# A fused decoder layer on one core: the causal mask of the score maxima added in row tiles, small VectorE steps in one-input forms, and the gate's last step on GpSimd

## The chip, the cores and the metric

The kernel runs on one core of one Trainium2 chip. The metric is the device time of one execution in microseconds. TensorE (PE), VectorE (DVE), ScalarE (ACT), GpSimd (POOL) and SyncE (SP, which only starts DMAs here) each run their own list of instructions in order and meet through semaphores.

## What is computed

64 sequences of 256 tokens with 256 features go through three attention layers and a gated feed-forward layer. All arithmetic is float32.

```
x = x + local_attention(layernorm(x))            # 16 heads of 16; a token sees its 7 neighbours
x = x + cross_attention(layernorm(x), ctx)       # keys and values: 120 rows of ctx
x = layernorm(x)
# decoder block:
a = einsum('bhqd,bhkd->bhqk', q, k) * hd ** -0.5         # q, k, v from rmsnorm(x, n1)
a = softmax(where(triu(ones, 1), -1e9, a))               # causal: no key later than the query
x = x + (a @ v) @ o_w.T
gp = softmax(xf @ gate_w.T); ew = top_k(gp, 2)           # xf = rmsnorm(x, n2)
ew = ew / (sum(ew) + 1e-9)
x = x + silu(xf @ up_w.T) @ down_w.T * sum(ew)
```

## The kernel before

One sequence at a time would leave the engines waiting for each other, so five sequences (LANES) are in work together. `sequence_parts` lists the parts of one sequence with an engine, an assumed duration and predecessors. `Plan` runs through all 64 sequences on a clock of its own with these durations and fixes three things before the program is built: the order of parts on each engine, which of four single PSUM banks (SINGLES) or of the one group of four banks (QUADS) each part fills, and the count that each wait needs. On the chip only the order and the waits remain. A changed duration, or a part on another engine, can therefore move parts that the edit does not name. In the steady state the order repeats once per sequence.

Parts that the text needs, with their lines:

- **Local layer, window path.** PE projects rows k, v, q (`project_rows`, L635), DVE adds biases (L1044), SP sends the rows to DRAM and fetches them back in windows of shifted tokens (`k_windows`, `v_windows`). POOL multiplies queries with windows in six k-chunks (L987), DVE reduces each (L1057), `window_max` (L1065 to L1069) centres them, ACT takes the exponent, `window_sum` (L1074 to L1077) normalises; then six v-chunks on POOL (L992).
- **Maxima.** The softmax needs each query's largest score. `max` fills the group of four banks with scores, one bank for each of the four row tiles of 32 contraction rows (L670; each matmul has a 32-row tile of TensorE to itself, so four run side by side), and DVE reduces them (L1100). For the causal layer (L677) a bfloat16 matmul of the identity with `causal_mask` adds -1e30 to later keys of the diagonal 128x128 block before the reduction. There are three fills per sequence: one of 128 queries with all 16 heads (512 columns of mask per bank), two of the other 128 queries with 8 heads each (256 columns).
- **`round_max`** (L1107 to L1109) splits the maxima into two bfloat16 parts, PE turns them (`shift`, L687), and `scores` (L700, L708) computes the scores again, keys by queries, with the maxima subtracted. ACT takes the exponent (L873), POOL zeroes later keys (`scores` on POOL, L1003), PE multiplies with the values (L731), `untangle` (L742, DVE L1117 and L1118) divides by the sums.
- **`turn_out`** (L756) transposes the attention result, ACT copies it (L898), `project_out` (L765) multiplies by the output weights, DVE adds it to x (L1129).
- **Feed-forward.** `gate` (PE L774, DVE L1133 to L1139, ACT L904, L906), `up` in four pieces (PE L784, ACT L917, DVE L1145), `weigh` (L1152 to L1156: sum of the two top weights over their sum plus 1e-9), `down` (PE L793, DVE L1161). `turn` (L617, ACT L834) transposes a normed input.

Every part that fills a bank waits until the engine that drains the bank's previous content is through. `settle` makes DVE or POOL wait for its own previous result.

## Time and profile before

| | before |
|---|---|
| median of 3 runs | 4210.85 us (4209.32 to 4218.56) |
| the profiled execution's own time | 4207.72 us |
| its span in the trace | 4206.0 us |
| busy share PE, DVE, ACT, POOL | 94%, 65%, 44%, 57% |
| TensorE's granted clock | 0.987 of full speed |

The span is the time from the first to the last traced instruction, 1.7 us less than that execution's own time, which in turn lies 3.1 us below the median. Busy shares are means over the whole span; with five sequences in flight an engine can be busy nearly all the time while what sets the pace runs through other engines.

### The profile page before, as it was taken

The page shows a single profiled execution, that of the slowest core. Times are in us where ns is not written, and L with a number is a line of the kernel's source. Part 1 is how long each engine was busy: PE and PEld are TensorE (multiplying, and loading weights), DVE is VectorE, ACT ScalarE, POOL GpSimd, SP SyncE. Part 2 cuts the span into 40 slices and gives each one's busy share as a digit, 9 for nine tenths or more (in the row PEclk, how much of TensorE's full clock was granted, in tenths as well). Part 3 has the DMA queues.
Part 4 walks back from the last instruction along what each step waited for, and adds up shares of the span by engine and source line. Part 5 has one row for each costly group of instructions (what it writes and reads, how often), then busy time and mean ns, then how long its engine had stood idle before and what let it go on. Part 6 is the DMA issues. An engine that isn't in the chain of part 4 may idle for free.

```text
span 4206.0 us, 92442 instructions
## 1 busy us (share of the span) xinstructions
PE 3943.8 (94%) x38016; PEld 3128.5 (74%) x38016; DVE 2745.3 (65%) x5137; ACT 1849.0 (44%) x3393; POOL 2402.4 (57%) x2898
## 2 busy tenths in 40 slices
PE   4699999999999999999999999999999999999997
PEld 4477777777777777777777777777777777777776
DVE  4666666666666766766766766766766766766742
ACT  1344444444444444444444444444444444444442
POOL 4655655655655655655655655655655556556521
PEclk9799999999999999999999999999999999999999
DMA  4111111111111111111111111111111111111100
GB/s 146 47 42 64 39 57 64 39 57 62 36 61 53 43 64 45 51 64 43 53 64 41 55 64 41 56 64 39 58 64 39 58 64 39 57 64 39 57 7 8
DMA packets 87125, 221.25 MB, mean 53 GB/s; under 512 B 8316, under 2 KB 53688, under 8 KB 70328
## 3 DMA queue, kind: packets, MB, share of 16 engines
q1 hardware_dynamic: 86712, 215.34, 14.3%
q8 instruction: 309, 5.06, 0.5%
q14 instruction: 104, 0.85, 0.1%
HBM read 164.92 MB, written 50.39 MB: 51 GB/s over the span
## 4 chain that ended last, share of the span: by engine, by line
PE 54%; POOL 18%; DVE 14%; DMA 7%; issue 3%; ACT 2%; SPq 0%; POOLq 0%; DVEq 0%
POOL chunks L987 11%; PE ps L793 11%; PE ps L651 9%; DMA k_windows<-passed_k 7%; PE ps L700 6%; PE ps L635 5%; PE ps L731 5%; PE ps L784 5%; PE ps L670 4%; DVE nmax L1100 3%; PE ps L617 3%; POOL x L960 2%; PE ps L657 2%; DVE nmax_parts L1107 2%; POOL x L965 2%
## 5 line engine op out<-in xcount | busy, mean ns | idle before, releaser
L992 POOL TENSOR_TENSOR chunks<-v_windows,xT 128x560 f32<-128x560 f32 (+1 forms) x384 | 868.0, 2277 | 386.5 <-DVE xT L1077 264.8
L1100 DVE TENSOR_REDUCE nmax<-ps 128x16 f32<-128x1920 f32 (+2 forms) x320 | 714.7, 2234 | 419.7 <-PE ps L670 283.2
L987 POOL TENSOR_TENSOR chunks<-rest,k_windows 128x512 f32<-128x512 f32 (+1 forms) x384 | 554.8, 1453 | 691.9 <-DMA k_windows<-passed_k 684.6
L873 ACT ACTIVATE prob<-ps 120x1024 f32<-120x1024 f32 (+1 forms) x512 | 619.7, 1236 | 739.2 <-PE ps L708 738.6
L784 PE MATMUL ps<-xT,w_up 128*128 128x256 f32 x2048 | 505.7, 391 | 58.7 <-ACT xT L834 44.0
L1003 POOL TENSOR_SCALAR_AFFINE_SELECT prob<-prob 128x512 f32<-128x512 f32 x512 | 314.0, 639 | 386.1 <-ACT prob L873 386.1
L784 PEld LDWEIGHTS ps<-xT,w_up 128*128 128x128 f32 x2048 | 377.8, 192 | 145.2 <-ACT xT L834 57.0
L793 PE MATMUL ps<-w_down,held 128*128 128x256 f32 x2048 | 459.1, 382 | 2.2 <-DVE held L1145 2.2
L1057 DVE TENSOR_REDUCE xT<-chunks 128x32 f32<-128x512 f32 (+1 forms) x384 | 293.4, 764 | 253.9 <-POOL chunks L987 248.7
L1057 DVE TENSOR_REDUCE held<-chunks 128x80 f32<-128x560 f32 (+1 forms) x384 | 296.2, 771 | 242.7 <-POOL chunks L992 237.7
L793 PEld LDWEIGHTS ps<-w_down,held 128*128 128x128 f32 x2048 | 383.8, 190 | 62.2 <-issue 9.4
L917 ACT ACTIVATE rest<-ps 128x512 f32<-128x512 f32 x256 | 152.7, 597 | 604.1 <-PE ps L784 604.1
L700 PE MATMUL ps<-held 32*120 32x256 f32 (+2 forms) x6144 | 391.1, 368 | 18.3 <-ACT prob L873 12.9
L670 PE MATMUL ps<-held 32*128 32x256 f32 (+2 forms) x8192 | 374.1, 313 | 20.8 <-DVE nmax L1100 8.3
L700 PEld LDWEIGHTS ps<-held 32*120 32x120 f32 (+1 forms) x6144 | 284.9, 184 | 137.8 <-issue 128.6
L670 PEld LDWEIGHTS ps<-held 32*128 32x128 f32 x8192 | 285.5, 187 | 83.4 <-issue 62.3
L731 PE MATMUL ps<-prob,va 120*32 120x256 f32 (+2 forms) x6144 | 332.1, 348 | 12.0 <-POOL prob L1003 3.3
L1035 DVE BATCH_NORM_STATS2 stats<-x 128x6 f32<-128x256 f32 x384 | 143.9, 417 | 231.9 <-DMA x<-in_x 229.8
L898 ACT COPY xT<-ps 128x512 f32<-128x512 f32 x128 | 74.9, 585 | 446.1 <-PE ps L756 446.1
L731 PEld LDWEIGHTS ps<-prob,va 120*32 120x32 f32 (+1 forms) x6144 | 185.0, 109 | 114.4 <-issue 61.2
L617 PE MATMUL ps<-ident,held 128*128 128x128 f32 x1024 | 165.1, 285 | 30.0 <-ACT held L829 15.7
L617 PEld LDWEIGHTS ps<-ident,held 128*128 128x128 f32 x1024 | 114.5, 142 | 96.4 <-issue 60.3
(139 smaller groups left out, 6889.6 us busy)
## 6 DMA issues: line engine op xcount, KB each, us to landing
k_windows<-passed_k SPq DMA_DIRECT2D x64, 1024.0 KB, 4.8
v_windows<-passed_v SPq DMA_DIRECT2D x64, 1024.0 KB, 6.9
...
```

The lines of the kernel that those rows point to most:

```text
L617: last = nc.tensor.transpose(ps[:, b, col:col + P], xn[s][:, tb, k * P:(k + 1) * P], ident[:])
L651: last = nc.tensor.matmul(ps[:, b, m * n:(m + 1) * n], wt[:, k, m * P:(m + 1) * P], src[:, k, 0:n], start=(k == 0), stop=(k == 1))
L670: last = nc.tensor.matmul(ps[:, first + r, place * keys:(place + 1) * keys], qT[s][e][rows, m, tb * P:(tb + 1) * P], kT[s][rows, m, 0:keys ...
L700: nc.tensor.matmul(ps[0:keys, first + r, n * T + col:n * T + col + qs], kT[s][rows, m, key0:key0 + keys], qT[s][e][rows, m, q0:q0 + qs], s ...
L731: last = nc.tensor.matmul(ps[SLOT * j:SLOT * (j + 1), b, e * T + q0:e * T + q0 + qs], va[s][0:keys, kb, head:head + SLOT], pr[0:keys, j, c ...
L784: last = nc.tensor.matmul(ps[:, b, m * T:(m + 1) * T], w_up[:, k, (2 * m2 + m) * P:(2 * m2 + m + 1) * P], xT[s][:, k, :], start=(k == 0), ...
L793: last = nc.tensor.matmul(ps[:, b, tb * D:(tb + 1) * D], hid[s][:, m, tb * P:(tb + 1) * P], w_down[:, m, :], start=(m == 0), stop=(m == F ...
L873: last = nc.scalar.activation(dst[0:keys], ps[0:keys, first:first + 4, n * T:n * T + dst.shape[2]], ACT.Exp, scale=SCALE)
L987: last = nc.gpsimd.tensor_tensor(chunk_of(c).rearrange("p (j d) -> p j d", d=D), q_row, window("k", (b + first) * D, (D, n), (1, D)), ALU. ...
L992: last = nc.gpsimd.tensor_tensor(chunk_of(c).rearrange("p (h i j) -> p h i j", i=HD, j=WINDOW), window("v", b * D + first * HD, (HD, n), ( ...
L1057: nc.vector.tensor_reduce(to, chunk_of(c).rearrange("p (x i) -> p x i", i=width), AX_X, ALU.add).then_inc(reduced[s], 1)
L1100: nc.vector.tensor_reduce(dst, src, AX_X, ALU.max, negate=True).then_inc(emptied[b], 1)
```

## The change

Five edits:

1. The mask of the maxima is added in row tiles. In setup PE builds two tables, `pick_rows` and `mask_rows`, which hold for each slab of 32 queries the selecting matrix and the mask's rows, repeated in each of the four row groups; DVE copies them out of PSUM as bfloat16. In a causal fill, each slab (0 to 3) and each row tile issue one matmul with 32 contraction rows, over the keys from 32 x slab on: 128, 96, 64 and 32 keys per head in place of 128 for every query.
2. `round_max` uses three reductions over an axis of length one (or two) in place of a cast, a subtraction and a cast. The gate's negation becomes such a reduction too.
3. `weigh` moves from DVE to POOL, with four instructions in place of five: fac = t * (t + 1e-9 z) ** -1. `down` on DVE waits for it through a new semaphore.
4. The durations that `Plan` assumes: 1.38 and 1.12 for PE in a causal fill (before 1.72 and 1.29), and `weigh` as 1.2 on POOL (before 0.9 on DVE).
5. Setup work: POOL makes one more 512-column pattern, PE eight matmuls, DVE two copies of 512 columns.

```diff
-                pe = 0.85 if layer == CROSS else 1.72 if tb == 0 else 1.29
+                pe = 0.85 if layer == CROSS else 1.38 if tb == 0 else 1.12
...
-    weighed = part("weigh", (), "DVE", 0.9, [a])
+    weighed = part("weigh", (), "POOL", 1.2, [a])
...
+            @block.tensor
+            def _(pe):
+                pe.wait_ge(setup_pool, 16)
+                for b, src in ((0, ident_b), (1, causal_mask)):
+                    for slab in range(4):
+                        last = nc.tensor.matmul(ps[:, b, slab * P:(slab + 1) * P], like_rows[:, slab, :], src[:],
+                                                start=(slab == 0), stop=(slab == 3), skip_group_check=True)
+                last.then_inc(setup_pe, 1)
...
-                dve.wait_ge(setup_dve, 24)
+                dve.wait_ge(setup_pe, 1)
+                for b, dst in ((0, pick_rows), (1, mask_rows)):
+                    nc.vector.tensor_copy(dst[:].rearrange("p s q -> p (s q)"), ps[:, b, :]).then_inc(setup_dve, 1)
+                dve.wait_ge(setup_dve, 26)
...
                         if L == CAUSAL:
-                            for r in range(4):
-                                to = ps[:, first + r, 0:2 * len(ms) * keys].rearrange("p (g k) -> p g k", k=keys)
-                                last = nc.tensor.matmul(to[:, :, tb * P:(tb + 1) * P], ident_b[:],
-                                                        causal_mask[:, 0:2 * len(ms), :], start=False, stop=True,
-                                                        skip_group_check=True)
+                            for slab in range(4):
+                                for r in range(4):
+                                    rows = slice(32 * r, 32 * r + 32)
+                                    to = ps[:, first + r, 0:2 * len(ms) * keys].rearrange("p (g k) -> p g k", k=keys)
+                                    later = mask_rows[rows, slab, 32 * slab:P].unsqueeze(1)
+                                    last = nc.tensor.matmul(to[:, :, tb * P + 32 * slab:(tb + 1) * P],
+                                                            pick_rows[rows, slab, :],
+                                                            later.to_broadcast([32, 2 * len(ms), P - 32 * slab]),
+                                                            start=False, stop=True, tile_position=(32 * r, 0),
+                                                            skip_group_check=True)
                         last.then_inc(filled[b], 1)
...
+                    elif name == "weigh":
+
+                        pool.wait_ge(exps_ready[s], reached["exps_ready", "gate", seq, ()])
+                        settle(nc.gpsimd.tensor_scalar(fac_r[s][:], zsum[s][:], 1e-9, None, ALU.mult))
+                        settle(nc.gpsimd.tensor_tensor(fac_r[s][:], tsum[s][:], fac_r[s][:], ALU.add))
+                        settle(nc.gpsimd.tensor_tensor(fac_r[s][:], fac_r[s][:], neg_one[:], ALU.pow))
+                        nc.gpsimd.tensor_tensor(fac[s][:], tsum[s][:], fac_r[s][:], ALU.mult).then_inc(weighed[s], 1)
                 for s in range(LANES):
+                    pool.wait_ge(weighed[s], plan.total["weighed", s])
...
                         hi, lo = half_max(s)[:, :, 0:4], half_max(s)[:, :, 4:8]
-                        whole = nmax[s][:].rearrange("p b (r g) -> p (b r) g", g=4)
-                        left = nmax_rest[s][:].rearrange("p b (r g) -> p (b r) g", g=4)
-                        settle(nc.vector.tensor_copy(hi, whole))
-                        settle(nc.vector.tensor_tensor(left, whole, hi, ALU.subtract))
-                        nc.vector.tensor_copy(lo, left).then_inc(nmax_ready[s], 1)
+                        whole, less = (nmax_pair[s][:, n].rearrange("p b (r g) -> p (b r) g", g=4) for n in range(2))
+                        both = nmax_pair[s][:].rearrange("p n b (r g) -> p (b r) g n", g=4)
+                        with nc.allow_low_precision(reason="the second part holds what the first one rounds off"):
+                            settle(nc.vector.tensor_reduce(hi, whole.unsqueeze(3), AX_X, ALU.max))
+                            settle(nc.vector.tensor_reduce(less, hi.unsqueeze(3), AX_X, ALU.max, negate=True))
+                            nc.vector.tensor_reduce(lo, both, AX_X, ALU.add).then_inc(nmax_ready[s], 1)
                     elif name == "shift":
...
-                        nc.vector.tensor_scalar(ntop[s][:], top[s][:, :, 0], -1.0, None,
-                                                ALU.mult).then_inc(tops_ready[s], 1)
+                        nc.vector.tensor_reduce(ntop[s][:], top[s][:, :, 0:1], AX_X, ALU.max,
+                                                negate=True).then_inc(tops_ready[s], 1)
...
-                    elif name == "weigh":
-
-                        dve.wait_ge(exps_ready[s], reached["exps_ready", "gate", seq, ()])
-                        settle(nc.vector.reciprocal(fac_r[s][:], zsum[s][:]))
-                        settle(nc.vector.tensor_tensor(fac[s][:], tsum[s][:], fac_r[s][:], ALU.mult))
-                        settle(nc.vector.tensor_scalar(zsum[s][:], fac[s][:], 1e-9, None, ALU.add))
-                        settle(nc.vector.reciprocal(fac_r[s][:], zsum[s][:]))
-                        settle(nc.vector.tensor_tensor(fac[s][:], fac[s][:], fac_r[s][:], ALU.mult))
                     elif name == "down":
                         b = bank(name, seq, args)
                         dve.wait_ge(biased[s], reached["biased", "norm", seq, (3,)])
+                        dve.wait_ge(weighed[s], reached["weighed", "weigh", seq, ()])
```

The planner's numbers move parts. Three places show it, with one turn of the repeating order picked out (a number behind a name is the lane's or buffer's, as in xT2); the line numbers of the change are higher by 26 to 40 (PE: L696 is the former L670, L706 L677, L773 L742, L805 L774, L815 L784, L787 L756, L796 L765, L643 L617, L683 L657, L677 L651, L731 L700, L739 L708, L762 L731).

First TensorE, at the last causal fill of a sequence and the feed-forward of the one ahead of it. Before:

```order
L670 MATMUL ps<-held1 128x256 x8
L677 MATMUL ps<-causal_mask,ident_b 128x2x128 x4
L742 MATMUL ps<-ident,rest2 128x128 x4
L774 MATMUL ps<-w_gate,xT0 128x8 x4
L784 MATMUL ps<-xT0,w_up 128x256 x4
L756 MATMUL ps<-ident,held2 128x128 x4
L765 MATMUL ps<-w_cross_o,xT2 128x256 x4
L784 MATMUL ps<-xT0,w_up 128x256 x4
L617 MATMUL ps<-ident,held3 128x128 x4
L784 MATMUL ps<-xT0,w_up 128x256 x4
L687 MATMUL ps<-ident_b,nmax_parts1 128x128 x2
```

and with the change:

```order
L696 MATMUL ps<-held1 128x256 x8
L706 MATMUL ps<-mask_rows,pick_rows 128x2x128 x4
L706 MATMUL ps<-mask_rows,pick_rows 128x2x96 x4
L706 MATMUL ps<-mask_rows,pick_rows 128x2x64 x4
L706 MATMUL ps<-mask_rows,pick_rows 128x2x32 x4
L773 MATMUL ps<-ident,rest2 128x128 x4
L805 MATMUL ps<-w_gate,xT0 128x8 x4
L815 MATMUL ps<-xT0,w_up 128x256 x4
L787 MATMUL ps<-ident,held2 128x128 x4
L815 MATMUL ps<-xT0,w_up 128x256 x4
L796 MATMUL ps<-w_cross_o,xT2 128x256 x4
L643 MATMUL ps<-ident,held3 128x128 x4
```

The mask is sixteen small matmuls; the third piece of `up` now stands ahead of `project_out` (w_cross_o), directly behind `turn_out`.

Second VectorE, from the end of `window_max` to `round_max`. Before:

```order
L1069 TENSOR_TENSOR xT2<-xT2,nmax2 128x224
L1117 RECIPROCAL rsum0<-ps 128x16
L1118 TENSOR_TENSOR held0<-ps,rsum0 128x256
L1074 TENSOR_REDUCE rsum2<-xT2 128x32
L1076 RECIPROCAL rsum2<-rsum2 128x32
L1077 TENSOR_TENSOR xT2<-xT2,rsum2 128x224
L1117 RECIPROCAL rsum0<-ps 128x16
L1118 TENSOR_TENSOR held0<-ps,rsum0 128x256
L1100 TENSOR_REDUCE nmax4<-ps 128x4x2
L1145 SCALAR_TENSOR_TENSOR held3<-rest3,ps 128x512
L1107 CAST nmax_parts4<-nmax4 128x8x4
L1108 TENSOR_TENSOR nmax_rest4<-nmax4,nmax_parts4 128x32
```

and with the change:

```order
L1108 TENSOR_TENSOR xT2<-xT2,nmax_pair2 128x224
L1157 RECIPROCAL rsum0<-ps 128x16
L1158 TENSOR_TENSOR held0<-ps,rsum0 128x256
L1139 TENSOR_REDUCE nmax_pair4<-ps 128x4x2
L1157 RECIPROCAL rsum0<-ps 128x16
L1158 TENSOR_TENSOR held0<-ps,rsum0 128x256
L1113 TENSOR_REDUCE rsum2<-xT2 128x32
L1115 RECIPROCAL rsum2<-rsum2 128x32
L1116 TENSOR_TENSOR xT2<-xT2,rsum2 128x224
L1147 TENSOR_REDUCE nmax_parts4<-nmax_pair4 128x8x4
L1148 TENSOR_REDUCE nmax_pair4<-nmax_parts4 128x32
L1149 TENSOR_REDUCE nmax_parts4<-nmax_pair4 128x8x4
```

The reduction of the last causal fill (nmax_pair4<-ps 128x4x2) now runs ahead of the second `untangle` and ahead of `window_sum`; `up` (held<-rest,ps) has gone behind `round_max`.

Third TensorE, behind `down`, from the turn of the next causal layer on. Before:

```order
L617 MATMUL ps<-ident,held2 128x128 x4
L756 MATMUL ps<-ident,held4 128x128 x4
L657 MATMUL ps<-w_cross_v,y4 120x256 x2
L700 MATMUL ps<-held1 128x256 x4
L700 MATMUL ps<-held1 128x128 x4
L708 MATMUL ps<-nmaxT1,pick 128x256 x4
L708 MATMUL ps<-nmaxT1,pick 128x128 x4
L731 MATMUL ps<-prob0,va1 32x256 x4
L731 MATMUL ps<-prob0,va1 32x128 x4
L731 MATMUL ps<-prob1,va1 32x256 x4
L731 MATMUL ps<-prob1,va1 32x128 x4
L700 MATMUL ps<-held1 128x256 x4
```

and with the change:

```order
L643 MATMUL ps<-ident,held2 128x128 x4
L683 MATMUL ps<-w_cross_v,y4 120x256 x2
L731 MATMUL ps<-held1 128x256 x4
L731 MATMUL ps<-held1 128x128 x4
L739 MATMUL ps<-nmaxT1,pick 128x256 x4
L739 MATMUL ps<-nmaxT1,pick 128x128 x4
L677 MATMUL ps<-xT2,w_causal_q 128x256 x4
L731 MATMUL ps<-held1 128x256 x4
L731 MATMUL ps<-held1 128x128 x4
L739 MATMUL ps<-nmaxT1,pick 128x256 x4
L739 MATMUL ps<-nmaxT1,pick 128x128 x4
L762 MATMUL ps<-prob0,va1 32x256 x4
```

`turn_out` of the local layer (L756) has left this place (it now stands behind the first causal fill and its `project_out`), and the projection w_causal_q, which stood behind the last scores, stands ahead of them; the `values` (prob,va) come after all four scores.

## Rows read from the trace of the kernel before

**Rows 1.** The page: busy time by engine; chain that ended last by line.

```profile
PE 3943.8 (94%) x38016; PEld 3128.5 (74%) x38016; DVE 2745.3 (65%) x5137; ACT 1849.0 (44%) x3393; POOL 2402.4 (57%) x2898
...
POOL chunks L987 11%; PE ps L793 11%; PE ps L651 9%; DMA k_windows<-passed_k 7%; PE ps L700 6%; PE ps L635 5%; PE ps L731 5%; PE ps L784 5%; PE ps L670 4%; DVE nmax L1100 3%; PE ps L617 3%; POOL x L960 2%; PE ps L657 2%; DVE nmax_parts L1107 2%; POOL x L965 2%
```

**Rows 2.** Chain of waits, one turn around 2000 us: start, duration (us), what.

```profile
1991.56 1.93 PE ps L635 x8
...
1996.86 4.73 DMA k_windows<-passed_k
...
2016.83 0.40 DVE xT L1065
...
2020.65 2.28 DVE nmax L1100
...
2023.53 1.42 DVE nmax_parts L1107
...
2026.12 0.64 PE ps L617 x4
...
2027.48 1.97 PE ps L784 x8
...
2054.42 1.93 PE ps L635 x8
```

**Rows 3.** Timeline of all engines, 2013 to 2034 us: start, duration, instruction, idle before.

```profile
2018.76 0.53 DVE L1074 TENSOR_REDUCE rsum<-xT 128x32 f32<-128x224 f32 x1
...
2020.02 0.25 DVE L1117 RECIPROCAL rsum<-ps 128x16 f32<-128x16 f32 x1
...
2020.88 0.63 PE L756 MATMUL ps<-ident,held 128*128 128x128 f32 x4
...
2022.28 1.97 PE L765 MATMUL ps<-w_cross_o,xT 128*128 128x256 f32 x8 [0.77 <-ACT xT L898]
...
2026.65 0.68 DVE L1129 TENSOR_TENSOR x<-x,ps 128x512 f32<-128x512 f32 x1
...
2029.28 0.28 PE L687 MATMUL ps<-ident_b,nmax_parts 128*128 128x128 bf16 x2
2029.36 0.73 POOL L939 TENSOR_TENSOR rstd<-ms,neg_half 128x2 f32<-128x2 f32 x1
...
2029.64 1.97 PE L651 MATMUL ps<-xT,w_cross_q 128*128 128x256 f32 x8
...
2032.19 2.53 DVE L1156 TENSOR_TENSOR fac<-fac,fac_r 128x2 f32<-128x2 f32 x1
```

**Rows 4.** Timeline of TensorE, 2059 to 2072 us.

```profile
2062.28 1.04 PE L677 MATMUL ps<-causal_mask,ident_b 128*128 128x512 bf16 x4
2063.15 1.89 PE L765 MATMUL ps<-w_causal_o,xT 128*128 128x256 f32 x8
...
2067.66 0.40 PE L708 MATMUL ps<-nmaxT,pick 32*120 32x256 bf16 x8
2067.99 1.99 PE L657 MATMUL ps<-w_causal_v,xT 128*128 128x256 f32 x8
```

**Rows 5.** Timeline of all engines, 2034 to 2057 us.

```profile
2041.19 0.60 PE L756 MATMUL ps<-ident,held 128*128 128x128 f32 x4
...
2041.63 1.03 PE L657 MATMUL ps<-w_cross_v,y 128*120 128x256 f32 x4
...
2043.81 1.51 PE L731 MATMUL ps<-prob,va 128*32 128x256 f32 x32
...
2046.46 1.45 ACT L873 ACTIVATE prob<-ps 128x1536 f32<-128x1536 f32 x1 [0.50 <-PE ps L708]
...
2047.98 1.22 POOL L1003 TENSOR_SCALAR_AFFINE_SELECT prob<-prob 128x512 f32<-128x512 f32 x2 [1.51 <-ACT prob L873]
...
2048.38 1.26 ACT L846 ACTIVATE held<-ps,half 128x512 f32<-128x512 f32 x2 [0.47 <-PE ps L651]
```

**Rows 6.** The first cast of `round_max`, line L1107: duration min/median/max (ns).

```profile
L1107 DVE CAST nmax_parts<-nmax x128: 168/173/1791, 116.4 to 4137.0; 128x32 bf16<-128x32 f32 x128
```

41 lines of the change are left out of this document (27 added, 14 removed).

## The prediction

> **What bounds the kernel now.** I start on the page. TensorE is busy 94% of the span, VectorE 65%, GpSimd 57% [rows 1]. That invites the reading that every nanosecond taken from TensorE shortens the run. The page's chain contradicts it: its largest entry is GpSimd's window chunks (L987, 11%), and the fetch of k_windows has another 7% [rows 1]. So I follow the chain of waits over one turn of the repeating order. From one start of project_rows for k (L635, 1991.56) to the next (2054.42) are 62.86 us [rows 2]. I cut the turn into three stretches:
>
> - **Stretch 1**, 1991.56 to 2016.83, 25.27 us: project k, DMA out, the fetch (4.73 us), six k-chunks on GpSimd with other GpSimd work between them, up to window_max (L1065) [rows 2]. All but the first two microseconds is not TensorE.
> - **Stretch 2**, 2016.83 to 2027.48, 10.65 us: VectorE through window_max, untangle, window_sum, untangle, the reduction of 2.28 us, the stalled cast (1.42 us), then turn (L617), a copy, and the last `up` (L784) [rows 2].
> - **Stretch 3**, 2027.48 to 2054.42, 26.94 us: TensorE without interruption, from `up` over `down` to the next project_rows [rows 2].
>
> Two of the three causal fills lie in stretch 1 by time, the third at the seam to stretch 2. In all of them TensorE runs beside the chain. That places the change: the mask is cheaper where TensorE is not on the path, and only what moves in stretches 2 and 3 counts. The order printed for both kernels repeats in 58 of 64 turns, so I multiply by 58.
>
> **The mask itself.** Before, four matmuls of 512 columns take 2063.15 - 2062.28 = 0.87 us, 0.22 each [rows 4]: 0.42 ns per column. In row tiles four matmuls run side by side: eight of 256 columns (L708), two rounds, take 2067.99 - 2067.66 = 0.33 us including the switch back to the undivided array [rows 4]. Two rounds of 256 at 0.42 ns are 0.22, so the switch costs 0.11. New 16-head fill: (512+384+256+128) columns x 0.42 = 0.54 us, plus the switch, now behind the mask and not ahead of it. Saved: 0.33. New 8-head fill: 640 columns, 0.27, against 0.43: saved 0.16, twice. Unknown is whether rounds of 128 and 64 columns keep that rate. Bounds: if each short round costs a full 256-column round (0.11 us), the 8-head fill takes 0.44 and saves nothing, and the 16-head fill still saves 0.28. I take 0.03 us per fill off for the shortest round, about 0.55 us per sequence in all. On the chain it is worth zero in my main case; its cover is TensorE's slack ahead of turn_out, worked out below as about 0.9 us. Without the cover it would be 0.55 x 64 = 35 us.
>
> The Trainium skill (TensorEngine Tiling (Array Packing), Performance Considerations) says a matmul has about 60 cycles of overhead, so very short ones gain nothing. By it the 64-column round is at its floor, and my 0.03 would be nearly nothing; no sum here changes.
>
> **round_max and the gate.** The cast takes 0.17 us at the median and up to 1.79 [rows 6], 1.42 in this turn [rows 2]; GpSimd's v-chunks run at that time. The three reductions are near the uncontended 0.2 us, 0.65 with their waits: 1.2 us less on VectorE in stretch 2. If reductions stalled too, round_max would stay at 1.85 us. The Trainium skill (SBUF — State Buffer, Who interferes with whom) says that a cast can take the port pair shared with GpSimd and then blocks, while `tensor_reduce` never contends. By that rule the stall is gone, by the other bound it stays; which of the two hardly moves the end, as the next part shows.
>
> **Stretch 2 with the new order.** Let W be window_max's start. VectorE before: window_max and the first untangle to W + 1.93 (window_sum starts 2018.76), window_sum 1.26 (to 2020.02), second untangle, and TensorE's turn_out at 2020.88, W + 4.05 [rows 3]. After: the reduction, about 2.20 from start to start (2.28 busy [rows 2]), stands there and window_sum behind. turn_out comes 2.20 - 1.26 = 0.94 later, W + 4.99. This is the late step of the new order. From turn_out on: copy on ScalarE until 2022.28, 1.40 [rows 3]; then the third `up`, 1.80, project_out, 1.73 (estimates, from the 1.93 of project k's eight matmuls [rows 2] less 0.1 to 0.2 for the switch there), and turn, 0.44 like its twin turn_out [rows 5]. So the last `up` starts at W + 10.36, with no wait: its bank was drained by the second `up`, no longer by project_out's addition, which ran at 2026.65 to 2027.33 [rows 3] and was what it waited for before, along with the 1.4 us copy. Before: W + 10.65. Gain 0.29 us. project_out's own bank needs the first `up` on VectorE, now behind round_max: ready at W + 7.4, needed at W + 8.2. With stalled reductions W + 8.6, and 0.4 of the gain is lost.
>
> **Stretch 3.** turn_out of the local layer leaves it: 2041.63 - 2041.19 = 0.44 [rows 5]. It goes to stretch 1, where TensorE has slack. The shift-to-projection seam (2029.28 to 2029.64, 0.36 for two short transposes [rows 3]) waited for the third `up` on VectorE; its bank now comes from `turn`: 0.25 less. Two restarts behind waits are gone with it, an estimate of 0.15 from the same 0.1 to 0.2. Against this: w_causal_q used to run between the last scores and the next fill of the four banks and hid the exponent (1.45 us [rows 5]). Now `values` does (1.51 [rows 5]), but ScalarE first evicts q (1.26 [rows 5]), so the banks come free about 0.4 us later than TensorE wants them; then `values` waits some 0.15 for GpSimd's masking (1.22 [rows 5]) of the last scores. Net 0.84 - 0.55 = 0.29 less.
>
> **Stretch 1.** GpSimd has the same parts in slightly different order: nothing. ScalarE's norm there is 0 to 0.3 us tighter; I take 0.
>
> **weigh.** VectorE loses five small instructions, the last of which stalled 2.53 us [rows 3], behind the last `up`, ahead of nothing on the chain. On GpSimd four take at most 0.73 each (the power, L939 [rows 3]), about 1.5 us, between v-chunks, which also start 2.8 us later (behind window_sum). GpSimd's wait for the k_windows fetch absorbs it; queued behind it are the maskings of the scores, and these have about 1.9 us of room before `values`.
>
> **Sum.** (0.29 + 0.29) x 58 = 34 us less. Setup adds two copies of 512 columns on VectorE at its end, 0.68 each like L1129 [rows 3]: 1.4 more. The tail, where one sequence runs alone, gains about 2. Together 34: own time 4207.7 - 34 = 4173.7, and with the median 3 above it about 4177.
>
> **Rivals.**
> - *TensorE is the bound after all* (20%). For it: 94% busy. Against: the chain leaves it for 36 of 63 us. Then mask and stretch gains add: (0.55 + 0.58) x 60 = 68 us, 4143. The Trainium skill (Perfetto Trace Analysis, Identifying the Most-Contended Engine) has this rule: the engine with the highest occupancy is the one to optimise first.
> - *More than that* (5%): fewer stalls let stretch 1 shrink; 4110.
> - *Nothing is left* (15%): ScalarE's norm in stretch 1 (0.3) and the exponent behind the q eviction (0.3 more than I count) eat both gains: 4203 to 4219.
> - *Slower* (18%): turn_out is 0.94 later, and the rest of stretch 2 does not give it back, because the last `up` still waits for a drain on VectorE. Then 0.94 - 0.29 = 0.65 x 58 = 38 us more, 4249. It decides once the wait there keeps more than 0.65 of its former 0.9.
> - *My case* (42%): 4177, own range 4150 to 4200.
>
> The range reaches from 4120 to 4240 and leaves out under 2 in 10. A measurement of this kernel tells about 0.2%, 8.4 us, from no change. Faster by more: 42 + 20 + 5, less a few at the edge, 65%; within: 16%; slower: 19%.
>
> **What would show it.** In the trace after: turns of 62.3 us; turn_out at W + 5.0; the third `up` after a wait of 0.77 for turn_out's copy; no wait of the last `up` behind L643; first reduction of round_max near 0.2 us; 16-head masks of 0.54 to 0.65 us; stretch 1 unchanged at 25.3. I am wrong if stretch 1 changes, if GpSimd's maskings arrive late at `values`, or if the last `up` waits at W + 11.

## The result and the profile after

The changed kernel takes 4175.45 us at the median of 4 runs (4169.04 to 4178.95), beside 4211.02 us of the kernel before on the same chip (4 runs, 4209.32 to 4218.56): ratio 0.991, 95% interval 0.9893 to 0.9928. The forecast was 4177 us. The profiled execution took 4175.73 us with a span of 4174.0. The total was met, in part by luck: the turns gained less than forecast, and the first sequences gained what no term had. The runs below also show that two of the prediction's readings were not right.

The page of the kernel after (busy time by engine; the chain that ended last by line), beside [rows 1]:

```profile
PE 3876.1 (93%) x40328; PEld 3131.7 (75%) x40328; DVE 2518.5 (60%) x4820; ACT 1848.0 (44%) x3393; POOL 2488.5 (60%) x3156
...
POOL chunks L1018 12%; PE ps L824 11%; PE ps L677 9%; DMA k_windows<-passed_k 7%; PE ps L815 6%; PE ps L661 5%; ACT prob L904 5%; PE ps L731 4%; DVE nmax_pair L1139 4%; PE ps L696 4%; PE ps L796 3%; PE ps L762 3%; POOL x L991 2%; POOL x L99
```

TensorE is busy 68 us less in all (the mask alone takes 38 of that, see mask only) and still 93% of a shorter span. The chain still has the window chunks first. New on it is ScalarE's exponent (L904) with 5%.

The chain of waits over one turn after, with the events of [rows 2]:

```profile
1971.02 1.93 PE ps L661 x8
...
1976.32 4.79 DMA k_windows<-passed_k
...
1996.37 0.40 DVE xT L1104
...
2033.49 0.64 PE ps L661 x2
```

A turn is 62.47 us here, 62.86 before. The fetch and the six k-chunks that make up stretch 1 are as they were.

TensorE's timeline after (start, duration, instruction) with the masks, beside [rows 4]:

```profile
1978.77 0.72 PE L706 MATMUL ps<-mask_rows,pick_rows 32*128 32x512 bf16 x16
1979.42 1.99 PE L796 MATMUL ps<-w_causal_o,xT 128*128 128x256 f32 x8
...
1996.44 0.46 PE L706 MATMUL ps<-mask_rows,pick_rows 32*128 32x256 bf16 x16
1996.82 0.66 PE L773 MATMUL ps<-ident,rest 128*128 128x128 f32 x4
```

The 16-head mask takes 1979.42 - 1978.77 = 0.65 us, the 8-head mask 0.38. In the prediction's terms 0.54 + 0.11 and 0.27 + 0.11: the short rounds keep the rate of the long ones.

The timeline of all engines in stretch 2 after, beside [rows 3]. window_max starts at W = 1996.37:

```profile
2001.36 0.63 PE L787 MATMUL ps<-ident,held 128*128 128x128 f32 x4 [0.86 <-DVE held L1158]
...
2002.39 0.18 DVE L1147 TENSOR_REDUCE nmax_parts<-nmax_pair 128x32 bf16<-128x32 f32 x1
2002.60 0.19 DVE L1148 TENSOR_REDUCE nmax_pair<-nmax_parts 128x32 f32<-128x32 bf16 x1
2002.64 4.72 POOL L1023 TENSOR_TENSOR chunks<-v_windows,xT 128x672 f32<-128x672 f32 x2 [7.02 <-DVE xT L1116]
...
2002.76 1.97 PE L815 MATMUL ps<-xT,w_up 128*128 128x256 f32 x8 [0.77 <-ACT xT L929]
...
2002.96 0.68 DVE L1185 SCALAR_TENSOR_TENSOR held<-rest,ps 128x512 f32<-128x512 f32 x1
...
2004.56 1.89 PE L796 MATMUL ps<-w_cross_o,xT 128*128 128x256 f32 x8
...
2006.29 0.60 PE L643 MATMUL ps<-ident,held 128*128 128x128 f32 x4
...
2006.72 1.89 PE L815 MATMUL ps<-xT,w_up 128*128 128x256 f32 x8
```

turn_out stands at W + 4.99, the third `up` at W + 6.39 after a wait of 0.77, project_out at W + 8.19, turn at W + 9.92, the last `up` at W + 10.35 without a wait. The first cast's successor (L1147) takes 0.18 us and ends 0.07 ahead of GpSimd's first v-chunk (2002.64); the second reduction (L1148) runs into that chunk and takes 0.19. Over the whole trace:

```profile
L1147 DVE TENSOR_REDUCE nmax_parts<-nmax_pair x128: 174/177/186, 118.8 to 4103.8; 128x32 bf16<-128x32 f32 x128
L1148 DVE TENSOR_REDUCE nmax_pair<-nmax_parts x128: 185/186/188, 119.0 to 4104.1; 128x32 f32<-128x32 bf16 x128
```

L1147 stands in the place of the line in [rows 6], whose longest was 1791 ns. By itself it doesn't show that a reduction escapes the stall, since by start times and durations only 4 of the 128 overlap with a GpSimd instruction. Of L1148 64 do, with the same 188 ns at most, and of the first reduction in forms only (below) 63 do, with 181 ns at most.

Stretch 3 after, beside [rows 5]:

```profile
2024.37 1.26 ACT L877 ACTIVATE held<-ps,half 128x512 f32<-128x512 f32 x2 [0.47 <-PE ps L677]
...
2025.53 1.45 ACT L904 ACTIVATE prob<-ps 128x1536 f32<-128x1536 f32 x1
...
2027.12 1.17 PE L696 MATMUL ps<-held 32*128 32x120 f32 x32 [0.32 <-ACT prob L904]
...
2028.52 1.51 PE L762 MATMUL ps<-prob,va 128*32 128x256 f32 x32 [0.23 <-POOL prob L1034]
```

TensorE waits 0.32 us for the four banks behind the last exponent and 0.23 for GpSimd's masking: the two waits that the prediction had put at 0.4 and 0.15. The exponent (to 2026.98) had to wait for q's eviction, as the prediction said.

Over many turns the same cuts give the following table. It is worked out from start times in each trace, as means over turns 8 to 57 of the repeating order: "to chunk" is from project_rows k to the first k-chunk, "chunks" from there to W. Means are longer than the typical turn, since the fetch of k_windows takes up to 3 us more in some.

| kernel | median us, ratio to before (95%) | turn | to chunk | chunks | W to last `up` | last `up` to rows |
|---|---|---|---|---|---|---|
| before | | 63.39 | 10.77 | 15.08 | 10.64 | 26.87 |
| after | 4175.45, 0.991 (0.9893 to 0.9928) | 62.93 | 10.74 | 15.10 | 10.38 | 26.70 |
| mask only | 4207.37, 0.9995 (0.9986 to 1.0003) | 63.40 | 10.77 | 15.09 | 10.64 | 26.88 |
| old mask | 4166.70, 0.9902 (0.9888 to 0.9915) | 62.73 | 10.50 | 15.19 | 10.34 | 26.70 |
| mask twice | 4188.05, 0.9934 (0.9919 to 0.995) | 63.11 | 10.66 | 15.40 | 10.34 | 26.70 |
| forms only | 4132.76, 0.9822 (0.9809 to 0.9835) | 62.12 | 10.77 | 15.09 | 9.41 | 26.84 |
| old forms | 4255.44, 1.0104 (1.009 to 1.0118) | 64.28 | 10.65 | 15.12 | 11.80 | 26.70 |
| untangle first | 4135.96, 0.9803 (0.9784 to 0.9823) | 62.21 | 10.66 | 15.10 | 9.73 | 26.70 |
| order only | 4466.98, 1.06 (1.0584 to 1.0615) | 67.79 | 10.62 | 15.17 | 11.76 | 30.22 |
| weigh planned | 4318.63, 1.0266 (1.0249 to 1.0283) | 65.31 | 10.71 | 15.11 | 10.42 | 29.07 |
| weigh back | 4173.99, 0.9903 (0.9889 to 0.9917) | 62.86 | 10.67 | 15.11 | 10.37 | 26.70 |
| numbers back | 4157.78, 0.9878 (0.9862 to 0.9893) | 62.50 | 10.51 | 15.10 | 9.40 | 27.49 |
| tight | 4230.11, 1.0053 (1.0039 to 1.0066) | 63.77 | 10.67 | 15.08 | 9.19 | 28.83 |
| mask and forms | 4125.21, 0.9797 (0.9784 to 0.9811) | 62.10 | 10.77 | 15.08 | 9.41 | 26.83 |

By phases the changed kernel gains 8.1 us ahead of the sixth project_rows k (280.0 to 271.9), 25.4 in the turns up to the 64th (3673.7 to 3648.3), and loses 1.6 behind it (252.3 to 253.9).

### The profile page after: what moved, and what is told of

Its sections match the earlier page's. It is cut to its first block, busy times and chain, and to the rows that moved or that the text cites. A ratio compares the mean times of both kernels' runs of the same rounds, so it can differ in the third digit from the quotient of the medians.

```text
span 4174.0 us, 96951 instructions
## 1 busy us (share of the span) xinstructions
PE 3876.1 (93%) x40328; PEld 3131.7 (75%) x40328; DVE 2518.5 (60%) x4820; ACT 1848.0 (44%) x3393; POOL 2488.5 (60%) x3156
## 4 chain that ended last, share of the span: by engine, by line
PE 49%; POOL 20%; DVE 10%; DMA 8%; ACT 7%; issue 4%; SPq 0%; POOLq 0%; DVEq 0%
POOL chunks L1018 12%; PE ps L824 11%; PE ps L677 9%; DMA k_windows<-passed_k 7%; PE ps L815 6%; PE ps L661 5%; ACT prob L904 5%; PE ps L731 4%; DVE nmax_pair L1139 4%; PE ps L696 4%; PE ps L796 3%; PE ps L762 3%; POOL x L991 2%; POOL x L996 2%; PE ps L643 1%
## 5 line engine op out<-in xcount | busy, mean ns | idle before, releaser
L1139 DVE TENSOR_REDUCE nmax_pair<-ps 128x16 f32<-128x1920 f32 (+2 forms) x320 | 715.2, 2235 | 514.8 <-PE ps L696 353.0
L904 ACT ACTIVATE prob<-ps 120x1024 f32<-120x1024 f32 (+1 forms) x512 | 619.6, 1236 | 464.8 <-PE ps L739 464.4
L815 PE MATMUL ps<-xT,w_up 128*128 128x256 f32 x2048 | 509.4, 393 | 74.8 <-ACT xT L929 45.2
L815 PEld LDWEIGHTS ps<-xT,w_up 128*128 128x128 f32 x2048 | 375.5, 193 | 159.5 <-issue 83.3
L731 PE MATMUL ps<-held 32*120 32x256 f32 (+2 forms) x6144 | 391.3, 368 | 29.7 <-ACT prob L904 24.4
L696 PE MATMUL ps<-held 32*128 32x256 f32 (+2 forms) x8192 | 373.8, 313 | 38.8 <-ACT prob L904 24.0
L731 PEld LDWEIGHTS ps<-held 32*120 32x120 f32 (+1 forms) x6144 | 285.1, 184 | 157.3 <-issue 148.0
L696 PEld LDWEIGHTS ps<-held 32*128 32x128 f32 x8192 | 286.1, 187 | 95.7 <-issue 74.4
L762 PE MATMUL ps<-prob,va 120*32 120x256 f32 (+2 forms) x6144 | 332.4, 349 | 17.7 <-POOL prob L1034 17.7
L762 PEld LDWEIGHTS ps<-prob,va 120*32 120x32 f32 (+1 forms) x6144 | 177.0, 110 | 115.7 <-issue 52.3
L853 ACT ACTIVATE held<-x,nmean,rstd 128x256 f32<-128x256 f32 x256 | 140.0, 595 | 181.6 <-POOL nmean L972 180.4
L1185 DVE SCALAR_TENSOR_TENSOR held<-rest,ps 128x512 f32<-128x512 f32 x256 | 175.2, 685 | 37.0 <-ACT rest L948 31.0
```

What stands on the lines that cost most here:

```text
L696: last = nc.tensor.matmul(ps[:, first + r, place * keys:(place + 1) * keys], qT[s][e][rows, m, tb * P:(tb + 1) * P], kT[s][rows, m, 0:keys ...
L731: nc.tensor.matmul(ps[0:keys, first + r, n * T + col:n * T + col + qs], kT[s][rows, m, key0:key0 + keys], qT[s][e][rows, m, q0:q0 + qs], s ...
L762: last = nc.tensor.matmul(ps[SLOT * j:SLOT * (j + 1), b, e * T + q0:e * T + q0 + qs], va[s][0:keys, kb, head:head + SLOT], pr[0:keys, j, c ...
L815: last = nc.tensor.matmul(ps[:, b, m * T:(m + 1) * T], w_up[:, k, (2 * m2 + m) * P:(2 * m2 + m + 1) * P], xT[s][:, k, :], start=(k == 0), ...
L904: last = nc.scalar.activation(dst[0:keys], ps[0:keys, first:first + 4, n * T:n * T + dst.shape[2]], ACT.Exp, scale=SCALE)
L1139: nc.vector.tensor_reduce(dst, src, AX_X, ALU.max, negate=True).then_inc(emptied[b], 1)
```

## The experiments

The diffs are cut to their core. They stand against the changed kernel, that of forms only against the one before. Where a kernel has the old mask (old mask, forms only, order only), GpSimd's pattern and TensorE's eight matmuls of the new setup stay in it, and one copy in place of two makes the wide mask table.

### What the mask is worth

**Mask only.** The planner's numbers, `weigh`, round_max and the gate as before; only the mask and its setup are new. The order of parts is that of before.

```diff
-                pe = 0.85 if layer == CROSS else 1.38 if tb == 0 else 1.12
+                pe = 0.85 if layer == CROSS else 1.72 if tb == 0 else 1.29
...
+                        settle(nc.vector.tensor_copy(hi, whole))
+                        settle(nc.vector.tensor_tensor(less, whole, hi, ALU.subtract))
+                        nc.vector.tensor_copy(lo, less).then_inc(nmax_ready[s], 1)
```

Expected: 

> The row-tile mask alone (with its setup); planner's numbers, weigh and round_max as before, so every engine has the order of before. Chain theory (the mask lies beside the chain in all three fills): the steady turn stays at 62.9 to 63.4 us, setup costs 1.4 to 2.4, start and tail give back 2 to 10; 4209 us, 4200 to 4213. Rival, TensorE is the bound: about 0.55 us per sequence, 4178.

Measured: 4207.37 us, ratio 0.9995. The turn has not moved by 0.02 us in any stretch. TensorE's busy time on the page is 3905.5 us for 3943.8, 0.60 less per sequence, and the kernel takes as long. So the saving is covered in this order, and the rival "TensorE is the bound" falls. The Trainium skill (Perfetto Trace Analysis, Identifying the Most-Contended Engine) says to optimise first the engine with the highest occupancy, and to judge TensorE by the busy share of its weight loads. That is 74% here [rows 1], still the highest, but this edit takes nothing out of it (3140.5 us for 3128.5), so the ratio speaks against the reading by matmul time and leaves the page's own measure untested.

**Old mask.** The changed kernel with the four 128-row matmuls per fill of before; their wide table is copied on VectorE in setup.

```diff
+                            for r in range(4):
+                                to = ps[:, first + r, 0:2 * len(ms) * keys].rearrange("p (g k) -> p g k", k=keys)
+                                last = nc.tensor.matmul(to[:, :, tb * P:(tb + 1) * P], ident_b[:],
+                                                        causal_wide[:, 0:2 * len(ms), :], start=False, stop=True,
+                                                        skip_group_check=True)
```

Expected: 

> The changed kernel in its own order, with the mask added as before (four matmuls of 128 contraction rows). Chain theory: the cover in front of turn_out hides the third fill, but in the new order ScalarE's norm for the GpSimd work of stretch 1 is tight, and the 16-head fill comes 0.33 us later in front of it: up to 0.3 us per turn, 4175 + 10 to 19 = 4185 to 4194. If the mask is wholly hidden: 4175. Rival, TensorE is the bound: 4175 + 35 = 4210.

Measured: 4166.70 us, ratio 0.9902, which overlaps with that of the change. The stretch of chunks is 0.09 us longer; the one ahead of it, with the fetch, varies between any two kernels by as much as here (0.24 shorter). Nothing of the mask's saving can be seen to reach the end in the new order either, where TensorE waits 0.86 us ahead of turn_out (2001.36 above).

**Mask twice.** Every causal fill adds its mask two times, which changes the added value to -2e30.

```diff
-                            for slab in range(4):
+                            for slab in (0, 1, 2, 3, 0, 1, 2, 3):
```

Expected: 

> The changed kernel with the row-tile mask issued twice (adds -2e30 and not -1e30 to later keys): 1.1 us more TensorE work per sequence. Chain theory: the 16-head fill's second half (0.54) delays ScalarE's norm in stretch 1, the 8-head ones (0.27 each) meet the wait of turn_out: 0.5 x 58 = 30 us, 4205, 4195 to 4212. If the mask is wholly hidden: 4175. Rival, TensorE is the bound: 1.1 x 60 = 66, 4241.

Measured: 4188.05 us, 12.6 above the changed kernel; by the ratios it is 10, and the two intervals overlap a little. Of the 1.1 us more per sequence (0.54 + 2 x 0.27, since a second switch isn't needed) the stretch of chunks shows 0.30, more than its spread between the other kernels (15.08 to 15.19). The cover is wider than I expected (4205 us), but it ends.

### What the forms are worth

**Forms only.** Only round_max and the gate's negation have the new forms; mask, planner's numbers and `weigh` are those of before, and so is the order.

```diff
-                            settle(nc.vector.tensor_copy(hi, whole))
-                            settle(nc.vector.tensor_tensor(left, whole, hi, ALU.subtract))
-                            nc.vector.tensor_copy(lo, left).then_inc(nmax_ready[s], 1)
+                            settle(nc.vector.tensor_reduce(hi, whole.unsqueeze(3), AX_X, ALU.max))
+                            settle(nc.vector.tensor_reduce(less, hi.unsqueeze(3), AX_X, ALU.max, negate=True))
+                            nc.vector.tensor_reduce(lo, both, AX_X, ALU.add).then_inc(nmax_ready[s], 1)
```

Expected: 

> Only the one-input forms of round_max and of the gate's negation; mask, weigh, planner's numbers and order of before. Chain theory: the 1.2 us of stall in round_max stand on the chain of before through the second `up` and the bank of `turn`; without them `turn` starts 0.31 us earlier, where TensorE gets there by itself, so 0.31 x 58 = 18 us: 4193, 4188 to 4200. Rival, TensorE is the bound (VectorE is 65% busy): 4211.

Measured: 4132.76 us, 60 below what I expected. The forms alone gain 77 us, more than twice what the whole change does. The timeline of this kernel, W = 1977.88:

```profile
1984.49 0.18 DVE L1132 TENSOR_REDUCE nmax_parts<-nmax_pair 128x32 bf16<-128x32 f32 x1
...
1986.42 0.68 DVE L1154 TENSOR_TENSOR x<-x,ps 128x512 f32<-128x512 f32 x1
...
1986.85 0.60 PE L641 MATMUL ps<-ident,held 128*128 128x128 f32 x4
...
1987.29 1.92 PE L808 MATMUL ps<-xT,w_up 128*128 128x256 f32 x8
1987.55 0.58 ACT L858 COPY xT<-ps 128x512 f32<-128x512 f32 x1
```

The last `up` stands at W + 9.41, 1.24 ahead of before. In [rows 3] project_out's addition ran from W + 9.82, here from W + 8.54: 1.28 earlier, the stall that is gone. So before, the whole stall of the cast stood on the chain: cast, addition, bank, last `up`. The prediction had named the copy of turn's result, 1.4 us with its gaps, as a second thing that the last `up` waited for, and the 0.31 us of my expectation is turn's own gain (W + 8.97 here, W + 9.29 before) passed on through that copy. Here the last `up` starts 0.44 after turn and ahead of that copy (1987.55): it doesn't depend on it.

**Old forms.** The changed kernel with round_max's cast, subtraction and cast.

```diff
-                            settle(nc.vector.tensor_reduce(hi, whole.unsqueeze(3), AX_X, ALU.max))
-                            settle(nc.vector.tensor_reduce(less, hi.unsqueeze(3), AX_X, ALU.max, negate=True))
-                            nc.vector.tensor_reduce(lo, both, AX_X, ALU.add).then_inc(nmax_ready[s], 1)
+                        settle(nc.vector.tensor_copy(hi, whole))
+                        settle(nc.vector.tensor_tensor(less, whole, hi, ALU.subtract))
+                        nc.vector.tensor_copy(lo, less).then_inc(nmax_ready[s], 1)
```

Expected: 

> The changed kernel with round_max as cast, subtraction and cast. As the prediction has it (same stall as before, project_out 0.4 late): 4175 + 23 = 4198. Closer look: round_max now runs just behind window_sum, at the moment GpSimd starts its 2.5 us v-chunk, so the subtraction stalls for the whole chunk, the first `up` leaves its bank 2.3 us later and project_out waits 1.7 us: 4175 + 1.7 x 58 = 4273. Rival, TensorE is the bound: 4175.

Measured: 4255.44 us. Its timeline, W = 1975.90:

```profile
1982.17 4.62 POOL L1023 TENSOR_TENSOR chunks<-v_windows,xT 128x672 f32<-128x672 f32 x2 [7.03 <-DVE xT L1116]
...
1982.35 2.39 DVE L1147 CAST nmax_parts<-nmax_pair 128x32 bf16<-128x32 f32 x1
1984.66 0.68 DVE L1183 SCALAR_TENSOR_TENSOR held<-rest,ps 128x512 f32<-128x512 f32 x1
...
1985.48 1.97 PE L796 MATMUL ps<-w_cross_o,xT 128*128 128x256 f32 x8 [1.22 <-DVE held L1183]
...
1987.72 1.89 PE L815 MATMUL ps<-xT,w_up 128*128 128x256 f32 x8
```

The second cast begins 0.18 us after GpSimd's first v-chunk and ends when that chunk is through, 2.39 us for 0.18 of work. The first `up` on VectorE stands behind it, project_out waits for its bank (1.22), and the last `up` comes at W + 11.8 in place of W + 10.35. The new order has put round_max directly behind window_sum, which releases the v-chunks: without the new forms it is 1% slower than before. The expectation's closer look (4273) had this mechanism, on the subtraction in place of the second cast; its 4198 by the prediction's terms was too low.

### What the new order is worth

**Untangle first.** One swap on VectorE: the cross layer's second `untangle` goes ahead of the last causal reduction.

```diff
+            if dve[i][0] == "max" and dve[i][2] == (CAUSAL, 2) and dve[i + 1][0] == "untangle" and dve[i + 1][2] == (CROSS, 1):
+                dve[i], dve[i + 1] = dve[i + 1], dve[i]
```

Expected: 

> The changed kernel with two neighbouring parts swapped in VectorE's order: the second untangle of the cross layer ahead of the reduction of the third causal fill; all other orders and banks as they are. Chain theory: turn_out no longer waits until W + 5.0 but follows the second `up` at about W + 4.0; project_out is then held by the first `up`'s bank until W + 7.5, so the last `up` starts at W + 9.7 and not W + 10.35: 0.68 us per turn, 4175 - 39 = 4136, 4125 to 4150. Rival, TensorE is the bound: its work is the same, only its waits (0.9) could go: 4175 to 4120 without the stop at 0.68. Rival, the delay of turn_out costs nothing: 4175.

Measured: 4135.96 us. TensorE's timeline, W = 1913.71:

```profile
1919.09 1.97 PE L819 MATMUL ps<-xT,w_up 128*128 128x256 f32 x8 [0.82 <-ACT xT L933]
...
1921.11 1.96 PE L800 MATMUL ps<-w_cross_o,xT 128*128 128x256 f32 x8
...
1923.35 1.89 PE L819 MATMUL ps<-xT,w_up 128*128 128x256 f32 x8
```

The third `up` moves from W + 6.39 to W + 5.38, and the last to W + 9.64. project_out is held until W + 7.40 by the bank of the first `up`. The late turn_out of the new order is thus worth 0.65 us a turn by the means of that stretch and 0.71 in this turn, as expected.

**Order only.** The planner's two numbers are new; mask, forms and `weigh` (VectorE) are those of before.

```diff
-    weighed = part("weigh", (), "POOL", 1.2, [a])
+    weighed = part("weigh", (), "DVE", 0.9, [a])
```

Expected: 

> Only the planner's two numbers for a causal fill are changed: mask, round_max, gate and weigh are those of before, weigh on VectorE. TensorE's and ScalarE's order come out exactly as in the change. Chain theory: the new order has round_max behind window_sum, where the old forms stall behind GpSimd's chunk (2.3 us), weigh stalls ahead of project_out's addition, and the mask is late in front of the norm: 4175 + 98 + 17, more with weigh: 4280 to 4340, so slower than before. Rival, the order is what makes the change fast: about 4185. Rival, TensorE is the bound: 4211.

Measured: 4466.98 us, 6% slower than before; the direction was as expected, the size beyond it. Behind the last `up` are 3.35 us more than before. The timeline there:

```profile
2008.06 2.12 POOL L1016 TENSOR_TENSOR chunks<-v_windows,xT 128x560 f32<-128x560 f32 x1 [1.46 <-DVE held L1081]
2008.13 2.07 DVE L1176 TENSOR_TENSOR fac<-tsum,fac_r 128x2 f32<-128x2 f32 x1
...
2010.83 0.69 DVE L1152 TENSOR_TENSOR x<-x,ps 128x512 f32<-128x512 f32 x1
...
2011.66 2.60 PE L675 MATMUL ps<-xT,w_cross_q 128*128 128x256 f32 x8 [2.13 <-DVE x L1152]
...
2014.19 1.67 PE L724 MATMUL ps<-held 32*128 32x256 f32 x16
...
2023.27 0.94 PE L724 MATMUL ps<-held 32*128 32x256 f32 x16
```

The planner has put `weigh` ahead of project_out's addition. Its first product waits for a v-chunk, and the cross query projection waits 2.13 us behind it. That is the larger part of the 3.35. The rest is TensorE's granted clock. It is 1.00 from 2008.0 to 2011.6, where TensorE is busy 1.53 of 3.6 us, then 0.73 until 2014.3 and 0.83 until 2020.0, a mixture of its two levels, and 1.00 again. At the lower level the same sixteen matmuls (L724) take 1.67 us in place of 0.94, and the projection 2.60 where weigh planned has 1.97. Over the whole run the granted clock is 0.973 here and 0.987 before: 0.027 x 4464 less 0.013 x 4206 is 66 us, an estimate of 1.1 us a turn.

**Weigh planned.** The changed kernel, forms included, with `weigh` in its old instructions on VectorE and the planner told so (the diff above and the five instructions).

Expected: 

> The changed kernel with weigh back on VectorE in its five instructions and the planner told so (0.9 on VectorE). The planner then puts it between the gate and project_out's addition, as in the kernel with the new order alone, where its product stalled 2.07 us behind a v-chunk and the cross query projection on TensorE waited 2.13 us for project_out's addition. The forms of round_max and the gate are the new ones. My theory: the stall of weigh stands on the chain there; the turn is 1.5 to 2.5 us longer than in the changed kernel, 4260 to 4320. Rival, weigh costs nothing wherever it stands, as it did behind the last up: 4175.

Measured: 4318.63 us. Timeline, at the same place:

```profile
2005.52 1.14 DVE L1184 TENSOR_TENSOR fac<-tsum,fac_r 128x2 f32<-128x2 f32 x1
...
2006.69 2.06 DVE L1185 TENSOR_SCALAR zsum<-fac 128x2 f32<-128x2 f32 x1
...
2010.01 1.97 PE L676 MATMUL ps<-xT,w_cross_q 128*128 128x256 f32 x8 [1.95 <-DVE x L1160]
```

Two stalls now, 1.14 and 2.06 us, and TensorE waits 1.95, of 2.37 more than in the changed kernel behind the last `up`; the granted clock, 0.981, is lower here too. With the new numbers the forms alone don't save the kernel; `weigh` has to leave VectorE, or to stand elsewhere:

**Weigh back.** The changed kernel with `weigh`'s five instructions on VectorE, placed by hand directly behind the last `up` and not by the planner.

```diff
+            self.order["DVE"].insert(self.order["DVE"].index(("up", p[1], (3,))) + 1, p)
```

Expected: 

> The changed kernel with weigh back on VectorE in its old five instructions, placed directly behind the last `up`; all other orders as they are. Chain theory: its 3.3 us with the stall have cover on VectorE, and GpSimd's 1.5 us less had cover too: 4175, 4171 to 4180. Rival (VectorE's load sets the pace): up to 3.3 us per sequence, 4175 + 50 or more.

Measured: 4173.99 us, no difference. In this order it is the place of `weigh` that decides, not the engine.

### Put together again

**Numbers back.** The changed kernel with 1.72 and 1.29 again in the planner, and nothing else.

Expected: 

> The changed kernel with the planner's two numbers for a causal fill as before (1.72 and 1.29), all else changed: row-tile mask, one-input forms, weigh on GpSimd. The order of parts is then that of before but for weigh. My theory (the forms gain all of it, the new order gives half back, mask and weigh are worth nothing): as fast as the kernel in which only the forms are changed, about 4131 us (4125 to 4137). Rival, the mask's saving comes out once the stall is gone, because TensorE is then nearer to being the bound: 0.55 x 58 = 32 us less, about 4100. Rival, weigh on GpSimd delays the v-chunks or the maskings in this order: 4140 to 4160.

Measured: 4157.78 us: faster than the changed kernel by 18, not by the 44 expected. The third case held. Timeline at the end of the v-chunks, W = 1984.63:

```profile
2001.92 0.71 POOL L1042 TENSOR_TENSOR fac_r<-fac_r,neg_one 128x2 f32<-128x2 f32 x1
...
2004.05 4.26 POOL L1023 TENSOR_TENSOR chunks<-v_windows,xT 128x560 f32<-128x560 f32 x2
...
2008.35 0.74 DVE L1096 TENSOR_REDUCE held<-chunks 128x80 f32<-128x560 f32 x1 [0.61 <-POOL chunks L1023]
...
2009.14 0.66 PE L787 MATMUL ps<-ident,held 128*128 128x128 f32 x4 [0.43 <-DVE held L1096]
```

Here `weigh` on GpSimd stands ahead of the last two v-chunks. The last ends at W + 23.7 (forms only: W + 22.0), and the local layer's turn_out waits 0.43 for it and has moved behind another projection: last `up` to project_rows is 27.49 us, 0.65 more.

**Mask and forms.** The same with `weigh` on VectorE in its five instructions, so that the order is that of before.

Expected: 

> Row-tile mask, its setup, and the one-input forms; the planner's numbers and weigh (five instructions on VectorE) as before, so that the order of parts is that of before. It differs from the kernel of the forms alone (4132.8 us) by the mask only, and from the kernel with the numbers back (4157.8 us) by weigh only. My theory: the 25 us between those two are weigh's, whose four instructions on GpSimd (1.9 us with their gaps) make the last v-chunk end 23.7 us after window_max in place of 22.0, so that turn_out of the local layer waits on TensorE; the mask is worth nothing in this order too. So 4131 us (4125 to 4138). Rival, the row-tile mask costs something where TensorE waits less: 4150 to 4160. Rival, the mask's 0.55 us a sequence come out now: about 4100.

Measured: 4125.21 us, ratio 0.9797: the lowest of all, though untangle first (0.9803) can't be told from it. So `weigh` on GpSimd costs the kernel above some 33 us by the medians. In the traces, whose spans are 27 apart, it is 23 in the turns and 6.7 behind the 64th project_rows (253.0 to 246.3), with the start 2.8 shorter. Against forms only (0.9822) the median is 7 us lower, with intervals that just touch, and the turns are alike: 62.10 us against 62.12. The start is 3.6 longer, 2.2 of it setup; the end behind the 64th project_rows is 8.9 shorter. That goes with the granted clock. The windows of forms only, near the end (length, busy time of PE, PEld, DVE, ACT, POOL, then PEclk, the granted clock):

```profile
4080.00:4086.00 6.00, 3.46 (x80) 2.47 (x80) 0.81 (x2) 3.49 (x3) 2.00 (x4) 0.97 0.14 45
4086.00:4092.00 6.00, 4.60 (x40) 3.12 (x40) 0.63 (x2) 0.59 (x1) 0.44 (x1) 0.50 0.00 0
4092.00:4100.00 8.00, 5.05 (x13) 3.24 (x12) 2.13 (x6) 0.59 (x1) 0.66 (x1) 0.50 0.00 0
```

TensorE is granted 0.50, the lower of its two levels (1.2 GHz), through the last sequence's `values` and what follows; in mask and forms the window 4086 to 4092 has 1.00 (busy 3.63) and 4092 to 4100 has 0.82. The same 32 matmuls of `values` took 2.82 us there and 1.54 here. Every kernel falls to the lower level for a stretch in its last sequence, and the stretches differ: 27.3 us from 4085.7 in forms only, 6.8 from 4097.2 in mask and forms, 10.2 from 4178.2 before, 20.5 from 4136.5 in the changed kernel. The last `values` is hit in forms only, numbers back, mask twice, untangle first and weigh planned. The mean granted clock behind the 64th project_rows is 0.93 in forms only and 0.97 in mask and forms; the missing 0.07 x 255 and 0.03 x 246 are 10 us apart, an estimate of the size of the 8.9. That is no work that the mask saved; whether the mask's timing brings the better clock about, or chance, one trace of each doesn't tell. The same holds for the 6.7 us at the end of numbers back (0.94).

**Tight.** Numbers back with three moves: the first `up` on VectorE ahead of the last causal reduction, project_out's addition ahead of a window reduction, and on TensorE the third `up` ahead of project_out.

```diff
+                dve.remove(up)
+                dve.insert(at, up)
...
+            if pe[i][0] == "project_out" and pe[i][2] == (CROSS,) and pe[i + 1][0] == "up" and pe[i + 1][2] == (2,):
+                pe[i], pe[i + 1] = pe[i + 1], pe[i]
```

Expected: 

> The kernel of numbers back with three moves in the stretch from window_max (W) to the last up: the first up on VectorE ahead of the last causal reduction (its bank is then free at W + 4.6 in place of W + 6.7), project_out's addition ahead of the next window_reduce, and on TensorE the third up ahead of project_out, where it fills the wait for turn_out's copy. Worked out: third up W + 4.6, project_out W + 6.3, turn W + 8.1, project_out's addition on VectorE until W + 8.9, last up W + 9.05 in place of W + 9.40. Gain 0.35 x 58 = 20 us: about 4111 (4105 to 4120). Rival, TensorE's own work is the bound by now: no gain, 4131. Rival, the last reduction and round_max, now 0.7 later, delay the shift and with it the rest: slower than numbers back, 4140 to 4170.

Measured: 4230.11 us, slower than before. The last `up` did come earlier, at W + 9.19, 0.21 ahead of numbers back, but behind it are 1.34 more:

```profile
1967.09 1.97 PE L828 MATMUL ps<-xT,w_up 128*128 128x256 f32 x8 [0.44 <-DVE x L1182]
...
1969.20 0.66 DVE L1198 SCALAR_TENSOR_TENSOR held<-rest,ps 128x512 f32<-128x512 f32 x1
...
1970.01 1.97 PE L690 MATMUL ps<-xT,w_cross_q 128*128 128x256 f32 x8 [0.84 <-DVE held L1198]
```

I had left the third `up` on VectorE behind two window reductions and the moments. Its bank is the next that TensorE needs, and the cross query projection waits 0.84 us for it; the rest of the 1.34 was not traced. The rival that I had named, a late shift, is not what happened.

## Why the prediction was right, and where it was not

- **What bounds the kernel.** Right. The three stretches describe every kernel in the table, stretch 1 is the same before and after (25.85 and 25.84 us by the table), and mask only refutes the rival with TensorE as the bound: ratio 0.9995 for 0.60 us less busy time per sequence. One reading was off: that the chain leaves TensorE for 36 of 63 us counts all of stretches 1 and 2, but TensorE has 4.1 us of the chain in stretch 1, not two, and the page of before gives it 54% of the chain, so the chain leaves it for about half of the turn.
- **The mask's own time.** Predicted 0.54 + 0.11 and 0.27 + 0.11, with 0.03 more per fill for the short rounds; the trace has 0.65 and 0.38, so the 0.03 did not show. Right within 0.03 us a fill. Worth zero in the turns: right in both orders. The cover of about 0.9 us ahead of turn_out is nowhere worked out in the prediction; the trace after has 0.86 there.
- **The forms' own time.** Right: 0.18, 0.19 and 0.22 us, 0.65 in all, never stalled. By the Trainium skill (SBUF — State Buffer, Who interferes with whom) `tensor_reduce` never contends while a cast can; the traces agree: of the first reduction in forms only 63 of 128 ran beside a GpSimd instruction, with 181 ns at most, and the cast that stood in its place before took over 1 us in 59 of 128.
- **"Which of the two hardly moves the end".** This step failed. Old forms shows 80 us between the two, and forms only a gain of 77. The prediction bounded the stalled case by before's stall of 1.42 and put 0.4 of the gain at risk. In the new order the cast meets the first v-chunk head on: 2.39 us, project_out at W + 9.58 for the predicted W + 8.6, last `up` 1.45 later.
- **Stretch 2, new order.** Each start was met within 0.03 us: W + 4.99, 6.39, 8.19, 9.92, 10.35 against 4.99, 6.39, 8.2, 9.9, 10.36. But the gain of 0.29 was read as the new order's own. It is the forms' 1.24, less about 0.95 that the new order takes back. turn_out's delay, 4.99 - 4.05, is as large, and untangle first shows 0.65 to 0.71 of it to be turn_out's alone; there the bank of the first `up` takes over. The prediction had both numbers, the 0.94 and the wait of the last `up` for the addition on VectorE, and didn't follow that wait back to the stalled cast ahead of the addition.
- **Stretch 3.** Predicted 26.65, the turns have 26.70. The two new waits were foreseen (0.32 and 0.23 for 0.4 and 0.15). Against the mean of before it is 0.17 gained, not 0.29. The old forms kernel, in the new order, has the same 26.70, so this gain is the order's.
- **weigh.** Right for this kernel (weigh back, 4173.99), for the reason given, room at its place. It holds for this place alone. To have `weigh` on GpSimd and not on VectorE costs 33 us with the planner's old numbers (numbers back against mask and forms; 23 of them in the turns), and saves 143 where the planner places it on VectorE with the new numbers (weigh planned).
- **The sum.** Predicted -34: turns -34, setup +1.4, tail -2. Measured -32 in the spans: turns -25.4, start -8.1, end +1.6. So the total is luck within about 9 us: the turns gained 8.6 less than forecast, the end missed its 2, and the first sequences made up for both without a term in the sum. The setup did cost 2.4 us. What gives the start its gain is not shown. Forms only has it too (280.0 to 271.9) and mask only doesn't (279.7), but old forms (274.8) and order only (276.8) have part of it without the new forms. TensorE's granted clock from 40 us to the sixth project_rows is 0.82 before and in mask only, 0.85 in the changed kernel and forms only, 0.84 in old forms and order only; 0.18 x 240 less 0.15 x 232 is 8 us, an estimate of the same size. At the end the changed kernel is at the lower level for 20.5 us where before is for 10.2.
- **The slower rival** had the right kind of cause, a wait for a drain on VectorE in stretch 2. It comes about with the old forms in the new order, but there project_out waits (1.22) and the last `up` doesn't, so that the time of 4255 us lies near the rival's 4249 is chance.

The change, taken apart along one path by the ratios to before: the forms alone -1.78% (forms only), the mask added -0.25% and outside the turns (mask and forms), `weigh` on GpSimd +0.81% (numbers back), the planner's new numbers +0.32% (the change). Together -0.9%. Outside the turns the granted clock has a share in these. By the turn's mean the same four are -1.27, -0.02, +0.40 and +0.43 us. In other words two of its four parts gave back more than half of what the forms had gained.
